# Attention and quantised feed-forward on one core: h's maximum by TensorE and VectorE, halved first tiles and a new order in the maximum search

## What is computed

```
def act_qdq(x):                       # one scale for the whole tensor
    scale = max(max(abs(x)) / 32767, 1e-12)
    return clip(round(x / scale), -32768, 32767) * scale
def lpbq_dequant(w): ...              # 4-bit weights, a scale per 32 inputs

x = x + attention(layernorm(x), ctx, Wq, Wkv)        # x: 2 x 2048 x 512
h = act_qdq(layernorm(x))
up = act_qdq(h @ lpbq_dequant(w_up).T)               # 512 -> 1536
gate = act_qdq(h @ lpbq_dequant(w_gate).T)
sig = fixed_qdq_u16(sigmoid(gate))
gate = act_qdq(gate * sig)
o = act_qdq(gate * up)
out = x + o @ lpbq_dequant(w_down).T                 # 1536 -> 512
```

## Time and profile before

| what | value |
|---|---|
| median of three runs | 903.24 us (902.84 to 904.98) |
| the profiled execution | 900.13 us, of which the profile's span is 898.3 us |
| granted clock, mean over the span | 0.994 |
| PE busy | 865.5 us, 96% |
| DVE, ACT, POOL busy | 651.1, 560.2, 157.4 us |

### The profile page before, as it was taken

How to read it: one execution, slowest core, us unless ns; L and a number is a source line. 1 busy time by engine, 2 the same in 40 slices (tenths; PEclk the granted TensorE clock), 3 DMA queues, 4 the chain that set the end, 5 groups by cost and what they waited for, 6 DMA issues and landing times.

```text
span 898.3 us, 11791 instructions
## 1 busy us (share of the span) xinstructions
PE 865.5 (96%) x4144; PEld 426.7 (47%) x4144; DVE 651.1 (72%) x918; ACT 560.2 (62%) x673; POOL 157.4 (18%) x160
## 2 busy tenths in 40 slices
PE   7999969999999999999999989999799989999998
PEld 5777544444444444444444434444344434444443
DVE  4879883754346243279997859856999997999892
ACT  2378875553553454489997859763789975555430
POOL 0099940089001950000000000000000000000000
PEclk9999989999999999999999999999999999999999
DMA  9822319775369649884339993799998897989872
GB/s 347 332 93 98 128 59 305 205 194 198 140 234 296 206 161 294 322 319 157 132 149 327 363 347 142 251 402 373 374 379 265 276 322 271 386 286 406 317 294 100
DMA packets 107548, 230.20 MB, mean 256 GB/s; under 512 B 47216, under 2 KB 47216, under 8 KB 105328
## 3 DMA queue, kind: packets, MB, share of 16 engines
q1 hardware_dynamic: 106352, 225.48, 70.8%
q10 hardware_dynamic: 1152, 4.19, 1.3%
HBM read 127.40 MB, written 92.27 MB: 245 GB/s over the span
## 4 chain that ended last, share of the span: by engine, by line
PE 66%; DVE 16%; issue 8%; DMA 6%; ACT 3%; SPq 0%; POOL 0%; DVEq 0%; ACTq 0%
PE ps L871 28%; PE ps L948 13%; PE ps L903 10%; PE ps L975 3%; DVE big L1596 3%; PE ps L804 3%; DVE big L1589 3%; PE ps L743 2%; PE ps L818 2%; DVE small L1523 2%; DMA big<-gate_park 2%; DMA product_park<-big 2%; DVE small L1511 2%; DVE big L1518 1%; PE ps L965 1%
## 5 line engine op out<-in xcount | busy, mean ns | idle before, releaser
L993 ACT ACTIVATE big<-ps 128x1024 f32<-128x1024 f32 (+2 forms) x166 | 138.7, 845 | 189.6 <-PE ps L871 102.8
L871 PE MATMUL ps<-big 128*128 (+1 forms) x1152 | 250.5, 381 | 2.3 <-DVE big L1460 2.3
L903 PE MATMUL ps<-big 128*128 (+1 forms) x1152 | 249.0, 379 | 2.3 <-ACT big L993 2.3
L871 PEld LDWEIGHTS ps<-big 128*128 128x128 f16 x1152 | 113.1, 98 | 139.4 <-issue 4.6
L903 PEld LDWEIGHTS ps<-big 128*128 128x128 f16 x1152 | 112.6, 98 | 138.5 <-issue 2.8
L1478 DVE TENSOR_REDUCE small<-big 128x1 f32<-128x1024 f32 x48 | 58.3, 1219 | 135.2 <-ACT big L993 135.1
L948 PE MATMUL ps<-big 128*128 128x512 f16 x576 | 125.1, 379 | 2.7 <-DVE big L1617 2.7
L683 POOL PARTITION_ALL_REDUCE small<-small x8 | 3.3, 410 | 509.3 <-DVE small L1558 181.5
L948 PEld LDWEIGHTS ps<-big 128*128 128x128 f16 x576 | 56.2, 98 | 71.1 <-issue 2.9
L929 PE MATMUL ps<-big 128*128 128x512 f16 x384 | 85.2, 383 | 4.5 <-ACT big L1223 4.5
L1529 DVE CUSTOM_DVE_ANT_0 big<-big,small 128x1024 f32<-128x1024 int16 x48 | 61.7, 1284 | 7.3 <-ACT big L1173 0.5
(11 more groups left out here) (101 smaller groups left out, 1008.9 us busy)
## 6 DMA issues: line engine op xcount, KB each, us to landing
big<-up_park SPq DMA_DIRECT2D x90, 512.0 KB, 6.5
up_park<-big SPq DMA_DIRECT2D x48, 512.0 KB, 3.9
gate_park<-big SPq DMA_DIRECT2D x42, 512.0 KB, 2.9
big<-gate_park SPq DMA_DIRECT2D x42, 512.0 KB, 5.7
sign_park<-big SPq DMA_DIRECT2D x48, 256.0 KB, 3.1
big<-in_x_dram SPq DMA_DIRECT2D x8, 1024.0 KB, 17.5
x_park<-big SPq DMA_DIRECT2D x8, 1024.0 KB, 3.9
product_park<-big SPq DMA_DIRECT2D x16, 512.0 KB, 5.8
```

What stands on the lines that cost most here:

```text
L871: mm = nc.tensor.matmul(ps[:, 2 * (n % 2) + j], w[:, a, k, o:o + P], XT[:, g, b, k], start=(k == 0 and a + b == 0), stop=(k == KC - 1 and ...
L903: mm = nc.tensor.matmul(ps[:, b + j], WU[:, a, k, o:o + P], XT[:, g, c, k], start=(k == 0 and a + c == 0), stop=(k == KC - 1 and c == 1))
L993: return nc.scalar.activation(dst, src, ACT.Copy)
```

## The change

- h's maximum. `all_max(1, "hmx", "hall")` on POOL goes. PE turns the column `hmx` into a row of PSUM, DVE takes the row's maximum and writes it 128 times into `h_row`, and PE turns that row back into a column of PSUM, `hall`, which `quant_scale` reads.
- Order of the gate weights. `W_ORDER` and `W_EARLY` leave two low halves, not five, before h's maximum. PE's loop turns 9 blocks, not 12; the last three are turned, copied and split between units 1 to 4 of group 0. POOL's last gate part goes behind the layer norm, and the layer norm's last power isn't waited for together with the one before. Five `keep_warm` products more stand behind the wait for `xinv_d`.
- Up weights. SP loads them after four parked units of group 0, not ahead of all; DVE's `block_max` for them stands after two more units.
- Last up unit. Its two banks are given separately, DVE takes both maxima from PSUM, and ACT copies the unit afterwards. `signs_given` gives two signs per unit throughout. `keep_warm` stands ahead of the wait for the copy, with 10 products for 12.
- Search. The first product, its integer, its half and its first-pass matmuls are cut in two; the first piece of the down weights (`WD_FIRST`) is loaded during the up stage. DVE's order becomes product t + 1, whole tile t, maximum of product t. ACT's even integers are one tile further ahead up to c = 40. POOL makes 5 of 24 halves (`POOL_HI`). Six of the eight stores move from ACT's queue to SP's (`STORE_D1`).
- Down. The first whole tile's integer, halves and matmuls are cut in two, and its low half goes ahead of `split_int(0)`.

```
+W_ORDER = (2, 3, 0, 1, 7, 8, 4, 5, 6, 9, 10, 11)
+W_EARLY = 2
+W_LAST = 9
+FAR = 40
+POOL_HI = (9, 11, 15, 17, 21)
+STORE_D1 = {29: 0, 32: 1, 39: 2, 41: 3, 47: 4}
...
 def signs_given(n):
     m = n - B_UNIT - 2
-    return 0 if m < 0 else min(2 * m if m <= 6 else 12 + 3 * (m - 6), NS)
+    return max(0, min(2 * m, NS))
...
 def slot_free(eng, c):
-    eng.wait_ge(o_mx, c + 1)
-    if c % 2 == 0:
-        eng.wait_ge(ph_d, c // 2 + 1)
+    if c % 2:
+        eng.wait_ge(o_mx, c)
+    else:
+        eng.wait_ge(o_mx, c + 2)
+        high_given(eng, c // 2)
...
 # SP
+        if g == 0 and n == 4:
+            sp.wait_ge(wt_lo, OC)
+            sp.dma_start(WN..., wu_in...).then_inc(wn_ld[1], 16)
...
+                sp.dma_start(WD_FIRST, wd_d...[:, :, 0:2]).then_inc(wd_ld[0], 16)
...
     for c in range(14, NU):
+        if c in STORE_D1:
+            store_d1(STORE_D1[c])
         fetch_up_c(c)
...
 # POOL
-    all_max(1, "hmx", "hall")
+    quant_weights(7, NBLK // 8, 0)
...
+    for t in POOL_HI:
+        product_given(pool, t)
+        ...
+        nc.gpsimd.tensor_scalar(halves[:, PART[t]], seat(2 * t), D1_SCALE, 1.0, ALU.mult, ALU.mult).then_inc(pool_ph, 1)
...
 # PE
+    keep_warm(8, ident, P, 7)
+    pe.wait_ge(col_max, 2)
+    nc.tensor.transpose(ps[0:1, 7, 0:P], col["hmx"], ident).then_inc(ht_mm, 1)
+    pe.wait_ge(ht_ev, TI + 1)
+    nc.tensor.transpose(col["hall"], h_row, ident[0:1, 0:1]).then_inc(col_all, 1)
...
+        if ... g == 0 and ... 1 <= n <= OC - W_LAST:
+            turn_weights(W_LAST + n - 1)
...
-    keep_warm(8, ident, P, 7)
+    pe.wait_ge(xinv_d, 1)
+    keep_warm(5, ident, P, 7)
     gate(0)
...
 # ACT, search
+    for t in range(NS):
+        if 2 * t + 4 <= FAR:
+            up_int(2 * t + 4)
+        elif FAR < 2 * t + 2 < NU:
+            up_int(2 * t + 2)
         up_int(2 * t + 1)
-        if t + 1 < NS:
-            up_int(2 * t + 2)
-        product_hi(t)
+        if t + 1 < NS and t + 1 not in POOL_HI:
+            product_hi(t + 1)
         if t >= 8 and t % UPG in (2, 4):
             take_d1(...)
...
 # DVE
     nc.vector.tensor_reduce(col["hmx"], hcol, AX.X, ALU.max).then_inc(col_max, 1)
+    dve.wait_ge(ht_mm, TI + 1)
+    linked(nc.vector.tensor_reduce(col["fin"][0:1], ps[0:1, 7, 0:P], AX.X, ALU.max))
+    nc.vector.tensor_copy(h_row, col["fin"][0:1].to_broadcast([1, P])).then_inc(ht_ev, 1)
     for c in W_ORDER[W_EARLY:W_EARLY + 2]:
         weights_lo(c)
     dve.wait_ge(col_all, 2)
...
     def up_max(n):
+        if n + 1 == NU:
+            for j in range(2):
+                dve.wait_ge(u_mm, NU + j)
+                nc.vector.tensor_reduce(ucol..., ps[:, 2 * ((n + 2) % 4) + j], ...).then_inc(u_mx, 1)
+            return
...
     for t in range(NS):
+        if t + 1 < NS:
+            split_product(t + 1)
+        whole_max(t)
+        product_given(dve, t)
+        nc.vector.tensor_reduce(ocol[:, 2 + t:3 + t], seat(2 * t), ...).then_inc(o_mx, 1)
```

More of the change, by code:

```diff
@@ L716, in _ @@
             rstd1(3)
-            for g in range(NG - 1):
+            for g in range(NG):
                 normalise(g)
@@ L845, in _ @@
             pe.wait_ge(pro_ev, 12)
-            for n in range(W_SLOT + OC):
+            for n in range(W_SLOT + W_LAST):
                 if n + 1 < NT:
@@ L861, in _, with keep_warm @@
                     turn_h(n - H_LAG)
+            def keep_warm(count, square, width, bank):
+                for _ in range(count):
+                    nc.tensor.matmul(ps[0:width, bank, 0:width], square, square, start=True, stop=True)
+            keep_warm(8, ident, P, 7)
[3 more added lines that the diff above has]
+            nc.tensor.transpose(col["hall"], h_row, ident[0:1, 0:1]).then_inc(col_all, 1)
             def unit(w, g, n, done):
@@ L885, in gate @@
                 product(WG, g, g_mm, g_ev)
-            def keep_warm(count, square, width, bank):
-                for _ in range(count):
-                    nc.tensor.matmul(ps[0:width, bank, 0:width], square, square, start=True, stop=True)
-            keep_warm(8, ident, P, 7)
+            pe.wait_ge(xinv_d, 1)
+            keep_warm(5, ident, P, 7)
             gate(0)
@@ L924, in first_pass @@
                         pe.wait_ge(wd_ld[n], 16)
-                    pe.wait_ge(ph_d, t + 1)
+                    if t == 0:
+                        for c in range(2):
+                            pe.wait_ge(ph_d, c + 1)
+                            for i in range(TI):
+                                for b in range(2):
+                                    nc.tensor.matmul(ps[:, b0 + i], halves[:, PART[t], c * 512 + i * P:c * 512 + i * P + P],
+                                                     WD_FIRST[:, b, c], start=(c + b == 0), stop=False)
+                        continue
+                    if t == UPG:
+                        pe.wait_ge(wd_ld[0], 32)
+                    high_given(pe, t)
                     for i in range(TI):
@@ L1072, in _ @@
             take_xT(0)
-            for n in range(W_SLOT + OC + 1):
+            for n in range(W_SLOT + W_LAST + 1):
                 if n + 1 < NT:
@@ L1263, in _ @@
             for q in range(NS):
-                down_hi(q)
                 if q == 0:
+                    for c in range(2):
+                        w = slice(c * 512, c * 512 + 512)
+                        act.wait_ge(oq_d, c + 1)
+                        nc.scalar.activation(hi_place(0)[:, w], Q[:, HALF[whole(0)], w], ACT.Copy).then_inc(ohi_d, 1)
                     down_int(2)
+                else:
+                    down_hi(q)
                 for m in (2 * q + 3, 2 * q + 4):
@@ L1487, in _ @@
             gate_max(0)
+            gate_max(1, units=range(2))
             linked(block_max(0, 1, wn_ld[1]))
@@ L1490, in _ @@
             common_scale(1, 2)
-            for g in range(1, 3):
-                gate_max(g)
+            gate_max(1, units=range(2, UPG))
+            gate_max(2)
             gate_max(3, 1)
```

205 lines of the change are left out of this document (146 added, 59 removed).

## The result

The changed kernel takes 906.83 us (905.1 to 912.35, 8 runs), the kernel before 903.23 us (900.64 to 904.98, 8 runs) beside it: ratio 1.0045, 95% interval [1.0028, 1.0062]. It is slower by 4 us, where 2.35 us less were forecast. The profiled execution is the slowest of the eight (912.35 us, span 910.5 us), so the profile of a second set of runs of the same kernel (e1, span 907.6 us) is read beside it.

The account below looks back on a forecast made before the run. PE was taken to bound the gate and up stages; in the search DVE, ACT and PE lay within 0.5 us of each other. The parts summed -0.7 - 1.55 - 0.1 + 0 = -2.35 us, giving 900.8 us, range 898.6 to 903.8.

Parts of the forecast that it names:

- The warm products ahead of the turn: Before h's scale: eight products, some three done when half clock ends at 123.9, the rest by 125.2; scale 0.4 us earlier.
- Part 1: h's maximum and the gate stage: -0.4 - 1.7 + 1.4 = -0.7 us, between -1.5 and +1.6.
- The clock at gate(0): Five added products before gate(0) fill PE's idle time, so the clock stays at 2.4 GHz: 1.7 us won, at worst 0.
- (a): Rival: the clock drops before gate(0) all the same; -0.7 becomes +1.0, time 902.5 us; chance 0.15.
- Three turns: Gate stage: three blocks turned inside the PE-bound stage, 12 transposes, 1.4 us lost, 1.8 with a gap at each change.
- Up weights at no cost: Gate stage: up weights start later, POOL ends at 237.0, ACT stands 5.7 us, PE's cover holds by 0.5 us; cost 0.
- Part 2: Last up unit: DVE takes the last bank itself, the copy moves behind; 1.55 us won, between 1.0 and 1.6.
- Part 3: Search: rounds of 3.46 us win 2.9 us, the start takes it back, int(47) late by 0.9; -0.1 us, bounds -1.5 and +1.5.
- Part 4: Down: first tile starts earlier, second stays 9.1 us after L1611, PE's gain becomes a wait; cost 0, between -0.3 and +0.5.
- (b): Rival: the search wins what its new order promises, 1.5 us more, time 899.3 us; chance 0.20.
- (c): Rival: POOL and DVE get in each other's way in five search rounds, 5.8 us lost, time 906.6 us; chance 0.08.
- (d): Rival: the up weights miss their cover by 2 to 3 us, time 901.8 to 903.8 us; chance 0.07.

Follow-up runs that it names:

- e3: The kernel before with only the last up unit in two banks, both maxima from PSUM, and two signs per unit: 902.63 us, ratio 1.0003.
- e8: As e3, but the down weights' loads set ahead of the last unit's store on SP's queue: 901.76 us, ratio 0.9992 against the kernel before.
- e11: The kernel before with last-unit and search parts, down weights' loads ahead of the last unit's store, no early piece, gate part as before: 906.76 us, ratio 1.0062.
- e17: The kernel before with five added warm products behind the scale of h, before gate(0), and nothing else: 901.52 us, ratio 0.999.
- e4: The kernel before with only the search and down parts of the change, early piece of the down weights included: 904.05 us, ratio 1.0017.
- e14: As e11, but the down weights' loads stand behind the last unit's store again: 902.95 us, ratio 1.0006 against the kernel before.
- e16: As e8, but with the signs spread as in the kernel before: 903.91 us, ratio 1.0021 against the kernel before.
- e18: The kernel before with e17's five warm products and e8's last unit, even signs and order of loads: 902.01 us, ratio 0.9995.
- e7: The kernel before with the search part, but old signs and without the early piece of the down weights: 903.43 us, ratio 1.0005.
- e10: The kernel before with twenty added warm products after the scale, to make gate(0) start later: 905.02 us, ratio 1.0047.
- e2: The kernel before with only the gate part: h's maximum, new order of the halves, late up weights, added keep_warm: 905.48 us, ratio 1.0054.
- e15: The changed kernel without the early piece of the down weights and nothing else: 905.17 us, ratio 1.0034 against the kernel before.
- e13: The whole gate part as in e2, without the eight warm products ahead of the column's turn: 904.09 us, ratio 1.0027 against the kernel before.
- e12: The changed kernel without the eight warm products and the early piece, down weights' loads ahead of the last unit's store: 907.06 us, ratio 1.0055.
- e5: The kernel before with only h's maximum made by PE and DVE, warm products included, old order of the halves: 908.82 us, ratio 1.0068.
- e9: As e5, without the eight warm products ahead of the column's turn: 903.45 us, ratio 1.0025 against the kernel before.
- e6: The kernel before with only the halves' new order, three turns in the gate stage, late up weights; h's maximum still on POOL: 908.27 us, ratio 1.0061.

## Why the prediction was wrong

**The warm products ahead of the turn (Part 1).** This is the step that failed. It let half clock end at 123.9, so that five of eight products would run at full clock and be done at 125.2. Measured: all eight at half clock, 3.62 us, and the column turned at 126.90. Of these 1.7 us, 0.9 are PE's turns before it, which started later in this execution (121.75 for 120.83). The rest of the step held: DVE's column came at 124.86 for 123.8, with the same 0.9 in it, and from the turn to the scale it took 2.11 us for 2.1.

The length of half clock in the earlier trace rows was taken for a constant of the kernel. It isn't one: around h's maximum, with the code there as before, it was 3.3 to 3.4 us in the kernel before, e3, e8, e11 and e17, 6.8 to 6.9 in e4, e14, e16 and e18, and 10.3 in e7 and e10. The bound of 0.5 us lost was too narrow as well: it was a bound on hand-offs, and the products' own time at half clock, twice 1.95, wasn't in it. The scale came 1.35 us later than before instead of 0.4 earlier.

What the products cost can be read in each profile as the time from the end of DVE's column to the start of the scale's reciprocal. It is 2.44 us in the kernel before. In the new order of the halves it is 3.24 (e2), 3.69 (e1), 4.50 (changed) and 4.51 us (e15) with them, 2.47 and 2.48 us without (e13, e12); in the old order 6.59 (e5) and 2.65 us (e9). So they cost 0.8 to 2.0 us in the changed kernel's order, and without them the new way is as long as POOL's. Undone, the step gives back 4 us in e9 (1.0068 to 1.0025) and 2.4 us in the gate part (1.0054 to 1.0027, intervals overlapping). No run takes the eight products alone out of the changed kernel, so their share of its 4 us is not shown.

**The clock at gate(0), 1.7 us.** It fell all the same, as rival (a) says. The term was wrong on the other side too: it counted a fall that two of eight profiles have, so it could at best be won in part of the runs. e17 bounds it: 0.9 us, between 1.8 and nothing.

**Three turns, 1.4 us.** Right: 5.61 - 5.18 = 0.43 us each, 1.3 in all.

**Up weights at no cost.** The path was read rightly, and the cover was missed by little. POOL ended at 241.05 (forecast 237.0, of which 1.3 us are gate(0)'s own lateness), ACT waited 6.42 us (forecast 5.7), PE 0.18. The wait that counted was another: 0.61 to 1.00 us at 176, behind turned transfers that share the DMA with the moved load. The step named them and gave no price. e13, in which gate(0) is 1.6 us earlier than before, still is 1.0027: in its stage stand 1.3 us for the turns and two waits of 0.73 and 0.78 us. Part 1 as a whole was forecast at -0.7 with bounds up to +1.6 and measured at +4.9.

**Part 2, 1.55 us.** Right in place and size: 4.3 to 2.7 us in e3. Wrong in that it was carried to the end: e3 is 1.0003. In its profile the search took 0.5 us more, the rest 1.3 us more with a stretch of half clock at its start, and PE waited 6.05 us for the down weights, whose loads the part itself had set behind a later store; the prediction didn't follow SP's queue past the late copy. The even signs are what it said: without them the first integer comes 2 us later (e16 against e8, one profile each).

**Part 3.** The round is 3.47 us (forecast 3.46), int(47) is late by 0.74 us (0.9), and the search alone is 0.4 (e7) to 1.1 us (e4) longer than before, for -0.1. Two sentences failed. One is that the early piece is hidden. It was loaded where the DMA share was 1.01, as it is there in the kernel before (1.03), and DVE's wait for signs behind it is 6.2 to 7.1 us with the piece and 4.1 to 5.3 us without; in e4 against e7 the first integer came 1.9 us later. Busy time by stretch of the changed kernel:

```profile
600.00:620.00 20.00, 19.99 (x94) 8.87 (x92) 15.30 (x21) 9.51 (x10) 0.00 (x0) 1.00 1.01 366
620.00:640.00 20.00, 19.69 (x104) 9.80 (x102) 12.19 (x16) 5.60 (x6) 0.00 (x0) 1.00 1.01 366
```

The other is that the stores on SP's queue have 5 us to spare. In the changed kernel DVE waited 0.53 and 0.59 us behind them, and its search is 1.1 us longer than before; in e7 DVE waited once, 0.51 us, and the search is 0.4 us longer; with the loads set ahead (e11, e12) the search was 3 us longer. Where no store was late the rounds were as forecast.

**Part 4.** The second whole tile came 9.6 us behind the first integer, for 9.1 forecast: the upper bound of its term.

**The rivals.** (a) happened and was priced with only the clock in it. (b) didn't. (c) had the right sign for the wrong reason, and that its 906.6 us stands next to the measured 906.83 is chance. POOL's halves are slow, DVE isn't; all instances in the changed kernel, min/median/max ns:

```profile
L778 POOL TENSOR_SCALAR big<-big x5: 2000/2015/2018, 677.7 to 720.6; 128x1024 f16<-128x1024 f32 x5
...
L1703 DVE TENSOR_TENSOR big<-big x23: 1211/1216/1220, 647.5 to 726.2; 128x1024 f32<-128x1024 int16 x23
```

(d) happened at a third of its price. No rival joined a late scale, a wait in the gate stage and a seam at which the DMA was full. Each was in the list of moved steps at 0 or within 0.5 us, and all their unpriced costs had one sign.

**What stays open.** PE's wait near 540 us, in the up stage, was 0.69 to 4.95 us. Of 11 profiles with 2.0 to 2.7 us four fall to half clock behind it (e9, e13, e17, e18), of four with 2.9 to 3.3 three, and of four with 3.5 and over all (e15, e6, e5, e1), for 3.4 or 6.9 us. All four of these hold edits of the gate part, but e2, e12 and e13 hold them too and waited 2.3 to 2.7 us, and e10 shows that lateness isn't the reason. It was not found why. Nor is it known what makes e2's other four runs 4 to 8 us slower than the profiled one.

## What to carry to other kernels

A warm product costs what the clock at its place makes it cost: put none ahead of an instruction on the path unless the row there shows PE at full clock. When a step is moved to a queue or a stretch with a DMA share near 1, price it by what else is waiting for data there, and never at nothing. A gain at one seam must be followed through the in-order queues to the next two waits, since here 1.6 us won at the maximum of u were lost again before the end.

## What the runs showed of the hardware

- POOL's half of 1024 columns took 2.02 us in all five cases, where 1.13 was worked out from the earlier trace rows. DVE's products beside it stayed at 1.22. In e11 POOL started at 700.83, 0.17 us behind DVE's two-input whole tile (700.66, 1.28 us), and ended at 702.85, 0.91 us behind that tile's end. The Trainium skill, page "SBUF — State Buffer", section "Who interferes with whom", says that the one that started first holds the shared port and the other waits. The trace agrees: in the changed kernel all five halves started 0.16 to 0.19 us behind such a whole tile, and none of the 24 whole tiles took over 1.29 us. How long the half takes alone no run shows.
- Where POOL changed from a reduction to other work or back with nothing else to wait for, it started 5.68 to 7.94 us after it was free, in all 20 profiles (5.78, 6.82, 6.13 and 7.14 in the rows above). The Trainium skill, page "GPSIMD Engine Reference", section "Instruction dispatch", gives about 6 us for the first call of a freshly loaded kernel. The trace agrees in size, not that it is the first call only: the time comes back at each such change. e6 shows that work put ahead of a reduction moves this time onto the path.
- Two turned transfers issued behind the load of the up weights took 9.06 to 10.16 us in seven profiles, against 2.5 to 3.6 us for the pairs after them.
